# Four graph layers in one pipeline: every engine's steps in another order, with other lags, and a wait in the first feed-forward product

## What is computed

```python
# layer 0: attention with q = k = v, 8 heads of 32, then a feed-forward part
normed = layer_norm(h, gamma1, beta1)
scores = einsum('bhqd,bhkd->bhqk', qkv, qkv) / sqrt(32)       # masked by adj > 0
x0 = h + softmax(scores) @ qkv
out0 = x0 + gelu(layer_norm(x0, gamma2, beta2) @ W1 + b1) @ W2 + b2
# layers 1 and 2: graph attention, 4 heads of 64
hh = h @ W;  e = leaky_relu(s_src[:, :, None] + s_dst[:, None, :], 0.2)
out12 = softmax(where(adj > 0, e, -big)) @ hh
# layer 3: attention with Wq, Wk, Wv, 4 heads of 64, mask adj | eye
out3 = relu((softmax(q @ k.T / 8) @ v) @ Wo + bo)
```

## Time and profile before

| | us |
|---|---|
| median of three executions | 4240.03 |
| lowest, highest | 4236.92, 4240.81 |
| profiled execution, span | 4240.1 |
| TensorE busy | 4042.6 (95%) |
| VectorE busy | 3223.4 (76%) |
| ScalarE busy | 2166.5 (51%) |
| GpSimd busy | 408.3 (10%) |
| moved by DMA | 193.90 MB, mean 46 GB/s |

### The profile page before, as it was taken

The page is one execution under the profiler, slowest core; times in us unless marked ns, Lnnn a source line. Parts: engine busy times, 40 slices in busy tenths (PEclk is TensorE's granted clock), DMA queues, the critical chain, the costliest instruction groups (busy, mean ns, idle before and its releaser), DMA issues.

```text
span 4240.1 us, 58963 instructions
## 1 busy us (share of the span) xinstructions
PE 4042.6 (95%) x22884; PEld 1929.7 (46%) x22884; DVE 3223.4 (76%) x6473; ACT 2166.5 (51%) x3361; POOL 408.3 (10%) x469
## 2 busy tenths in 40 slices
...
GB/s 99 29 42 50 56 37 49 34 53 51 56 36 51 31 53 52 56 36 51 31 52 54 56 35 51 31 51 56 56 32 54 31 51 56 56 31 46 21 31 31
DMA packets 212311, 193.90 MB, mean 46 GB/s; under 512 B 144448, under 2 KB 179008, under 8 KB 203584
## 3 DMA queue, kind: packets, MB, share of 16 engines
...
## 4 chain that ended last, share of the span: by engine, by line
PE 90%; DVE 5%; ACT 4%; DMA 1%; issue 1%; SPq 0%; POOL 0%; POOLq 0%; ACTq 0%; DVEq 0%
PE O L477 12%; PE M L425 11%; PE M L438 10%; PE S L358 6%; PE S L524 6%; PE O L371 6%; PE M L491 6%; PE O L540 6%; PE M L449 6%; PE O L481 5%; PE M L502 3%; PE M L416 3%; PE M L582 3%; PE O L382 2%; ACT PP L625 2%; PE M L398 2%
## 5 line engine op out<-in xcount | busy, mean ns | idle before, releaser
L1014 DVE SCALAR_TENSOR_TENSOR PG<-g,tcg,mT 128x512 f32<-128x512 f32 x1024 | 691.2, 742 | 33.1 <-PE O L481 21.4
L625 ACT ACTIVATE PP<-S,reach 128x1024 f32<-128x1024 f32 x512 | 542.6, 1111 | 318.8 <-PE O L371 114.5
L906 DVE TENSOR_TENSOR PP<-PP,mT 128x1024 f32<-128x1024 f32 x512 | 597.3, 1218 | 16.5 <-ACT PP L625 16.0
L477 PE MATMUL O<-PG,V 128*32 128x512 f32 x4096 | 550.9, 602 | 18.5 <-DVE PG L1014 17.0
L425 PE MATMUL M<-hT,W 128*128 128x512 f32 x1024 | 460.6, 603 | 3.1 <-ACT hT L660 2.8
L438 PE MATMUL M<-W,H 128*128 128x256 f32 x2048 | 459.7, 378 | 0.0
L438 PEld LDWEIGHTS M<-W,H 128*128 128x128 f32 x2048 | 377.3, 189 | 71.7 <-issue 10.6
L1126 POOL TENSOR_SCALAR ve<-mv 128x4 f32<-128x4 f32 x192 | 97.8, 509 | 3197.4 <-DVE mv L864 3197.4
L358 PE MATMUL S<-hT 32*128 32x512 f32 x2048 | 301.3, 658 | 30.8 <-ACT PP L625 29.4
L739 ACT ACTIVATE PP<-S,sh 128x1024 f32<-128x1024 f32 x256 | 272.1, 1118 | 87.5 <-DVE Q L916 49.0
L603 ACT ACTIVATE V<-z,nb,rs 128x256 f32<-128x256 f32 x128 | 76.6, 602 | 467.4 <-DVE nb L896 467.4
...
## 6 DMA issues: line engine op xcount, KB each, us to landing
g<-t_rows SPq DMA_DIRECT2D x64, 1024.0 KB, 4.7
adj<-adj_in SPq DMA_DIRECT2D x32, 1024.0 KB, 5.5
...
mT<-z SPq DMA_TRANSPOSE x128, 2.5
m<-V SPq DMA_TRANSPOSE x128, 2.5
```

What stands on the lines that cost most here:

```text
L477: e.matmul(k.O[0][r:r + 32, :], s.V[:, jt, 64 * hh + 32 * v:64 * hh + 32 * v + 32], p[:, u, :], start=(jt == 0), stop=(jt == NT - 1))
L625: e.activation(p[:, 2 * pair:2 * pair + 2, :], k.S[:, 2 * pair:2 * pair + 2, :], ACT.Exp, bias=k.reach[:, 7:8], scale=SC0).then_inc(k.e0.s ...
L906: e.tensor_tensor(p[:, 2 * pair:2 * pair + 2, :], p[:, 2 * pair:2 * pair + 2, :], s.mT[:, jt:jt + 1, :].to_broadcast([128, 2, N]), ALU.mul ...
L1014: e.scalar_tensor_tensor(out=p[:, u, :], in0=s.T[hh], scalar=s.tcg[:, 1, hh, jt:jt + 1], in1=s.mT[:, jt, :], op0=ALU.max, op1=ALU.mult).th ...
```

## The change

All five programs get another order of the same steps, and the batches lag by other numbers of iterations (a batch index `b1` of before is mostly `b3` now, and the loop runs from 3; on ScalarE and VectorE the loop body is also cut at another place). `Pe.w1` gets a wait for the weights' semaphore. No instruction is added or removed otherwise. The core of the diff, of the three long programs only the new side at the places that matter; what moved stands in words below it:

```diff
@@ Pe.w1
         e, k, s = self.e, self.k, self.k.of(b)
+        self.wait_ge(k.w_kept, 16)
         self.wait_ge(*k.hv[0].at(b, 1))
@@ gpsimd_program
-    for it in range(1, NB + 4):
-        b1, b2, b3, b4 = it - 1, it - 2, it - 3, it - 4
-        do.gmax(b3, 1)
-        do.rs(b4, 5)
-        do.rs(b3, 4)
-        do.rs(b1, 0)
-        do.rs(b2, 2)
-        do.gmax(b3, 2)
-        do.rs(b1, 1)
-        do.rs(b2, 3)
+    for it in range(0, NB + 2):
+        b0, b1, b2 = it, it - 1, it - 2
+        do.rs(b0, 0)
+        do.rs(b0, 1)
+        do.rs(b1, 3)
+        do.gmax(b1, 1)
+        do.rs(b2, 5)
+        do.rs(b1, 4)
+        do.rs(b0, 2)
+        do.gmax(b1, 2)
@@ sync_program
-    for it in range(1, NB + 6):
-        b1, b2, b3, b4, b5, b6 = it - 1, it - 2, it - 3, it - 4, it - 5, it - 6
-        do.store(b6)
-        do.load(b2)
-        do.masks_t(b2, 0)
-        do.masks_t(b2, 1)
-        do.loada(b1)
-        do.trow(b4, 2)
-        do.tbc(b4, 2)
-        do.rrow(b5)
-        do.rbc(b5)
-        do.trow(b3, 1)
-        do.tbc(b3, 1)
+    for it in range(2, NB + 6):
+        b2, b4, b6 = it - 2, it - 4, it - 6
+        do.loada(b2)
+        do.rrow(b6)
+        do.rbc(b6)
+        do.trow(b4, 1)
+        do.tbc(b4, 1)
+        do.store(b6)
+        do.load(b2)
+        do.masks_t(b2, 0)
+        do.trow(b4, 2)
+        do.tbc(b4, 2)
+        do.masks_t(b2, 1)
@@ tensor_program, body of the new loop
+    for it in range(3, NB + 6):
+        b3, b4, b5, b6 = it - 3, it - 4, it - 5, it - 6
...
+        do.pj(b5, 2, 2)
+        do.pj(b5, 2, 3)
+        do.prep_b(b4)
+        do.dn3(b6, 0)
+        do.pv3(b6, 2)
+        do.tt(b4, 0, 0)
...
+        do.gpv(b5, 2, 0)
+        do.gpv(b5, 2, 1)
+        do.rd3(b6)
+        do.tt(b4, 1, 0)
+        do.tt(b4, 1, 1)
+        do.gpv(b5, 2, 2)
+        do.pj(b4, 1, 0)
...
+        do.sc0(b3, 4)
+        do.qk(b5, 2)
+        do.dn0(b3, 1)
+        do.pv0(b3, 3)
+        do.sc0(b3, 5)
...
@@ scalar_program, parts of the new loop
+    for it in range(3, NB + 6):
...
+        do.out0(b4, 0)
+        do.sc0(b4, 5)
+        do.sq3(b6, 0)
+        do.lnz(b5, 2, 0)
+        do.qk(b6, 3)
+        do.vp(b6, 0)
+        do.lnz(b5, 2, 1)
+        do.sc0(b4, 6)
+        do.sq3(b6, 1)
+        do.lnz(b5, 2, 2)
+        do.lnz(b5, 2, 3)
+        do.sc0(b4, 7)
...
+        do.sc3(b6, 3)
+        do.pj(b5, 2, 2)
+        do.ln2(b4, 0)
+        do.ln2(b4, 1)
+        do.ln2(b4, 2)
+        do.ln2(b4, 3)
+        do.pj(b5, 2, 3)
+        do.tt(b4, 0, 0)
+        do.tt(b4, 0, 1)
+        do.gprep(b5, 2)
...
+        do.w1(b4, 7)
+        do.ln0(b3, 0)
+        do.ln0(b3, 1)
+        do.out3(b6, 1)
+        do.ln0(b3, 2)
+        do.ln0(b3, 3)
+        do.ln1(b3, 0)
+        do.ln1(b3, 1)
+        do.lnz(b4, 1, 0)
+        do.lnz(b4, 1, 1)
+        do.lnz(b4, 1, 2)
+        do.lnz(b4, 1, 3)
+        do.rd3(b6)
@@ vector_program, parts of the new loop
+    for it in range(2, NB + 6):
+        b2, b3, b4, b5, b6 = it - 2, it - 3, it - 4, it - 5, it - 6
+        do.pa3(b6, 2)
+        do.gprep(b5, 2)
+        do.bag(b3, 0, 1)
+        do.bst(b3, 0, 2)
+        do.masks(b3, 1)
+        do.pa3(b6, 3)
+        do.bag(b3, 0, 2)
+        do.gvals(b5, 2)
+        do.gw(b5, 2, 0)
+        do.gw(b5, 2, 1)
+        do.prep_w(b4)
+        do.bst(b3, 0, 3)
+        do.bag(b3, 0, 3)
+        do.nb(b3, 0)
+        do.bst(b3, 1, 0)
+        do.bst(b3, 1, 1)
+        do.w2(b4, 0)
...
+        do.pj(b4, 1, 1)
+        do.rb3(b6)
+        do.pj(b4, 1, 2)
+        do.pj(b4, 1, 3)
+        do.gmax(b4, 1)
+        do.gprep(b4, 1)
+        do.zb(b3)
+        do.gvals(b4, 1)
+        do.diag(b3)
+        do.wo(b6, 0)
...
+        do.sc0(b3, 7)
+        do.pa0(b3, 3)
+        do.bst(b2, 0, 0)
+        do.sc3(b5, 0)
+        do.masks(b2, 0)
+        do.rc(b3, 0, 0)
+        do.b2r(b3, 0, 0)
+        do.pa3(b5, 0)
+        do.sc3(b5, 1)
+        do.rc(b3, 0, 1)
+        do.fin(b3, 0, 0)
+        do.b2r(b3, 0, 1)
+        do.rc(b3, 0, 2)
+        do.bst(b3, 2, 0)
+        do.b2r(b3, 0, 2)
+        do.fin(b3, 0, 1)
+        do.fin(b3, 0, 2)
+        do.rc(b3, 0, 3)
+        do.bag(b3, 2, 0)
+        do.b2r(b3, 0, 3)
+        do.pa3(b5, 1)
+        do.bst(b3, 2, 1)
+        do.fin(b3, 0, 3)
+        do.bst(b3, 2, 2)
+        do.bst(b3, 2, 3)
+        do.bag(b3, 2, 1)
+        do.bag(b3, 2, 2)
+        do.bag(b3, 2, 3)
+        do.prep_b(b3)
+        do.pj(b4, 2, 0)
+        do.pj(b4, 2, 1)
+        do.sc3(b5, 2)
+        do.nb(b3, 2)
+        do.sc3(b5, 3)
+        do.pj(b4, 2, 2)
+        do.pj(b4, 2, 3)
+        do.bst(b2, 0, 1)
+        do.resid0(b3)
+        do.bag(b2, 0, 0)
+        do.gmax(b4, 2)
```

More of the change, by code:

```diff
@@ L1229, in tensor_program @@
 def tensor_program(do):
-    for it in range(1, NB + 4):
-        b1, b2, b3, b4 = it - 1, it - 2, it - 3, it - 4
[L1233 to L1302, removed]
-        do.pv0(b1, 3)
-        do.qk(b3, 2)
-        do.sc0(b1, 5)
-        do.dn0(b1, 1)
-        do.qk(b3, 3)
-        do.vp(b3, 0)
-        do.sc0(b1, 6)
-        do.pv0(b1, 4)
-        do.sq3(b3, 0)
-        do.pv0(b1, 5)
-        do.dn0(b1, 2)
-        do.sc0(b1, 7)
-        do.sq3(b3, 1)
-        do.pv0(b1, 6)
-        do.sc3(b3, 0)
-        do.tt(b2, 2, 0)
-        do.tt(b2, 2, 1)
-        do.pv0(b1, 7)
-        do.vp(b3, 1)
-        do.dn0(b1, 3)
-        do.sc3(b3, 1)
-        do.b2r(b1, 0, 0)
-        do.b2r(b1, 0, 1)
-        do.pv3(b3, 0)
-        do.sc3(b3, 2)
```

445 lines of the change are left out of this document (206 added, 239 removed).

## The result

The changed kernel takes 4248.17 us (median of seven, 4245.10 to 4262.91) beside 4240.03 (4236.92 to 4240.89) for the kernel before: ratio 1.0029, 95% interval 1.0017 to 1.0040. Forecast were 4229 us and a gain; by the medians it is slower by 8.1 us.

What follows compares the result with a forecast made beforehand. TensorE, busy 124.95 of 127.63 us a period, was taken as the bound. -21.8, 29 periods x (0.1 + 0.05 + 0.28) = +12.5, -3 at the start and +1 for first iterations gave -11.3: 4229 us, range 4212 to 4260.

Steps and rivals of the forecast that it cites:

- Part 4: Attention stretch: bag(0,2,3) 1.25 us later, partly regained; tt(0,0) +0.05 us a period, bounds 0 and 1.0.
- Part 1: rd3 before tt(1,0) on TensorE: its 0.73 us wait for bank M1 goes, 30 times, -21.8 us.
- Part 2: Projection pj(1) later by gpv(2,2), rb3 between its halves: 0.1 us a period, bounds 0 and 0.6.
- Part 3: After the output step: gw(1,0) 0.4 us late, absorbed by TensorE's next wait; 0 taken, bounds -0.1 and +0.2.
- Part 5: w1 stage: GpSimd's all-reduce 0.5 us later makes grow(2) wait; +0.28 us a period, bounds 0 and 1.0.
- Part 6: Queues and w2 stage: g lands 4.7 us after issue, w2(0) keeps 2 us of slack; cost nothing.
- Part 7: New wait in w1: prep_b(0) already waits for the same semaphore and value, so nothing is emitted; cost 0.
- Part 8: The ends: diag behind zb lets the first statistics end earlier, -3 us at the start; last periods 0.
- D: Rival: GpSimd's power instruction caught by both sc3(2) multiplications, 1.2 us later; about 1.4 us a period, 4259 us; chance 0.15.
- C: Rival: the gain returns as other waits, 0.8 us a period together; 4238 to 4242 us; chance 0.23.
- L416 waiting for V or stt by 0.5 us or more: Sign of a wrong forecast: TensorE's tt(0,0) waits that long for its data.

Runs made afterwards that it cites:

- k11_pa3b: The kernel before with only the pair sum pa3(1) of group 3 moved ahead of the statistics of group 2 on VectorE; 4270.77 us, ratio 1.0071.
- r7_rd3: The kernel before with rd3 moved as in the changed kernel and rb3 ahead of pj(1,2) on VectorE; 4230.50 us, ratio 0.9977.
- r2_rd3: The kernel before with rd3's move, but rb3 left behind zb and gprep on VectorE; 4253.00 us, ratio 1.0029.
- r6_pa3: The changed kernel with only pa3(1) put back behind the statistics of group 2 on VectorE; 4216.39 us, ratio 0.9940.
- r3_block: The kernel before with only VectorE's order in the output block as in the changed kernel; 4234.67 us, ratio 0.9981.
- r1_block: The changed kernel with only VectorE's order in the output block put back as in the kernel before; 4259.28 us, ratio 1.0045.

## Why the prediction was wrong, step by step

**Part 4 is the step that failed.** It had seen that pa3(1) ahead of the statistics makes bag(2,3) 1.25 us late, and then took nearly all of it back: GpSimd's first instruction would shrink from 1.11 to 0.23 us, and ScalarE would be done sooner with its copies. The instruction took 1.25: the two small copies that it was to meet were over when it started, and it ran beside a mask multiplication instead (1992.71 beside 1992.66). The two instructions together took 3.2 us from start to end as before, and GpSimd was 1.0 late. Part 4 looked for the price at tt(0,0)'s data, with a slack of 0.25. What came there was a wait for the bank, by way of VectorE's 0.93 us at nb(2) (0.33 us an iteration in k11_pa3b, 0.59 in the changed kernel), and the all-reduce, which follows GpSimd's second instruction after a nearly constant pause, carried the whole lateness to grow(2). Taken was +0.05 us an iteration with bounds of 0 and 1.0; k11_pa3b measured +28.6 us, 1.0 an iteration, on its own, and taking it out of the changed kernel gave 32. The range's end was right and the choice within it was not: the one row that priced it, 1.11 us in the earlier trace rows, was set aside for 0.23 us that no row of this place showed.

**Part 1** had the mechanism right (no wait on L569, none in its place at tt(1)) and the size too large: -0.49 us an iteration instead of -0.73, for the two further changes between kinds of products. As a whole it measured -10.0 us (r7_rd3) instead of -21.8, part 2's cost within.

**Part 2** counted 0.1 us an iteration. No steady wait came; single iterations lost up to 1.8 us for Gp (4.8 us over the run). Its remark that rb3 "just fits" is borne out by r2_rd3, where 2.1 us later costs 1.36 us each time.

**Part 3** was put at 0 (-0.1 to +0.2). Measured: -0.43 us an iteration by VectorE's denser order, of which the clock takes back 0.24 (r6_pa3) to 0.40 (the changed kernel) at the fourth scores product, -7.8 us net (r3_block). It had the direction of TensorE's waits right; that VectorE would be faster with the same instructions, and that the clock would answer to the waits, it did not see.

**Part 5** had the way to grow(2) right (GpSimd's instruction, the all-reduce 5.81 us later, the GELU, the bank) and its lateness wrong: 0.5 us at the all-reduce, 0.28 of it a wait. It gives no source for the 0.5, which is about what part 4's shortened GpSimd instruction leaves of 1.25 us; measured was 1.0. resid0 and the steps beside it cost next to nothing: with pa3(1) back and resid0 where the change put it (r6_pa3), tt(0,0) to grow(2) takes 6.49 us instead of 6.43 and grow(2) waits for H once.

**Part 6**: g landed in 5.0 us, and the only trace of w2 late is 0.2 us in L436: right. **Part 7** is not tried by itself; TensorE has the same 22884 products and no new wait at w1 in the list, which agrees. **Part 8**: the first qk product starts at 275.25 instead of 282.31 us, -7.1 where -3 was expected; r3_block alone has it at 279.39 and r7_rd3 at 278.73, 2.9 and 3.6 us earlier, so these two edits can account for most of it. But r1_block, the changed kernel without the new block order, has it at 273.90, so the parts do not simply add at the start, and diag alone was not tried: the cause of this gain stays open.

**The sum, measured.** Singly in the kernel before: -10.0 (rd3) -7.8 (block) +28.6 (pa3(1)) = +10.8 us, beside +8.1 for the whole change. The forecast had -21.8 + 2.9 (parts 1 and 2), 0 (part 3), 1.5 + 8.1 (parts 4 and 5, both of them the way of GpSimd's lateness) and -2 for the ends. The three were off by +9, -8 and +19 us. The two smaller errors nearly cancel, which is luck; what is left of the miss is the third. The rest of the change was not tried by itself: r6_pa3, all of it but pa3(1)'s move, is 24 us faster than the kernel before, 6 more than the 17.8 of rd3 and block singly, and what gives these 6 stays open.

**The rivals.** D named the nearest thing to what happened, with 4259 us. Its start was wrong: GpSimd's second instruction took 1.86 us, not over 3, and GpSimd was late from its start on. Its way on from there was right, step by step: nb holds up sc3(3) on VectorE, and the projection's copies, tt(0,0) and grow(2) follow, at 1.0 us an iteration instead of 1.4. The rule that speaks for D ("SBUF — State Buffer" in the Trainium skill, section "SBUF: two separate sides") would have added steps of 1.2 us to that chain; its length stayed at 3.2. The rows do not speak against the rule: beside VectorE's mask multiplications GpSimd's first instruction ended 0.1 us and its second 0.9 us behind the end of a whole VectorE instruction, 30 times each in k11_pa3b. C (the gain comes back as waits of TensorE, by parts 2, 4 and 5 together 0.8 us a period) describes the kind and nearly the size, with 1.0 us coming back, but of a gain that was smaller than it took it to be. Among the signs listed against the forecast, "L416 waiting for V or stt by 0.5 us or more" is the one that came.
